# Attention scores in pairs of units, and the probabilities' products at the end of their position

## What is computed

```python
q, k = _rope(_rms_norm(q, q_norm_w), _rms_norm(k, k_norm_w), cos, sin)
attn = jnp.einsum('bhqd,bhkd->bhqk', q, k) * scale
attn = jax.nn.softmax(jnp.where(causal, -jnp.inf, attn), axis=-1)
out = jnp.einsum('bhqk,bhkd->bhqd', attn, v)
x = _layernorm(x + out.transpose(0, 2, 1, 3).reshape(Bc, Tc, C) @ w_proj.T)
x = _layernorm(x + shared_expert(x) + two_of_eight_experts(x))   # abbreviated
```

## Time and profile before

| | us |
|---|---|
| Time, median of 3 runs | 952.51 |
| Time of the profiled execution | 957.52 |
| Its span from the first to the last instruction | 955.8 |
| Busy: PE / PEld / DVE / ACT / POOL | 896.0 / 693.3 / 576.6 / 615.3 / 457.2 |
| Sequences 1 to 6, from 79 us to 329 us | 250 |
| Rest after 370 us (last rows of attention's output, experts, output) | 586 |

### The profile page before, as it was taken

One profiled execution on the slowest core, in us unless ns is written; L12 is line 12 of the kernel. 1 busy time (PEld: TensorE's weight loads), 2 busy tenths in 40 slices (PEclk: granted clock), 3 DMA queues, 4 the chain that ended last, 5 costly groups with the idle time before them and its releaser, 6 DMA issues.

```text
span 955.8 us, 26112 instructions
## 1 busy us (share of the span) xinstructions
PE 896.0 (94%) x9049; PEld 693.3 (73%) x9050; DVE 576.6 (60%) x1152; ACT 615.3 (64%) x1060; POOL 457.2 (48%) x668
## 2 busy tenths in 40 slices
PE   4789999998999989999999999999999999999995
PEld 1444555555555546888889989989899889898885
DVE  8655698889888636784344444454444433428875
ACT  4788898888878766442656655556655453667753
POOL 5344557877878636572134444344434343412211
PEclk9799999999999989999999999999999999999998
DMA  5112223433212255567882122121212121248641
GB/s 175 67 68 95 94 101 106 158 114 135 101 58 84 69 176 194 202 204 266 267 292 74 50 67 70 52 68 55 67 56 67 46 68 47 74 145 269 214 160 44
DMA packets 68706, 112.76 MB, mean 118 GB/s; under 512 B 7728, under 2 KB 46000, under 8 KB 68496
## 3 DMA queue, kind: packets, MB, share of 16 engines
q1 hardware_dynamic: 51248, 77.32, 24.5%
q10 hardware_dynamic: 10896, 16.40, 5.9%
q0 software_dynamic: 6480, 17.97, 5.2%
HBM read 66.58 MB, written 45.08 MB: 117 GB/s over the span
## 4 chain that ended last, share of the span: by engine, by line
PE 76%; ACT 7%; DVE 6%; issue 4%; POOL 2%; DMA 2%; another core or an unknown queue 1%; ACTq 1%; DVEq 0%; SPq 0%; POOLq 0%
PE hb L1811 23%; PE yb L1827 23%; PE pv_bank L1599 6%; PE slot L1577 4%; PE ma L1612 4%; PE slot L1586 3%; PE hb L1665 3%; ACT prob L872 2%; PE mb L1747 2%; PE ma L1622 1%; PE tr L1685 1%; DMA rs<-resid 1%; PE yb L1702 1%; PE mb L1735 1%
## 5 line engine op out<-in xcount | busy, mean ns | idle before, releaser
L1042 ACT ACTIVATE hf<-hb,b 128x256 f32<-128x256 f32 (+1 forms) x392 | 155.0, 454 | 206.2 <-PE hb L1811 200.7
L1811 PE MATMUL hb<-xgT,wts 128*128 128x256 f16 (+1 forms) x1872 | 213.2, 263 | 1.4 <-ACT hf L1042 1.2
L1827 PE MATMUL yb<-wts,hh 128*128 x1704 | 210.5, 273 | 0.9 <-DVE hh L1454 0.9
L1454 DVE TENSOR_TENSOR hh<-hf,hh 128x1024 f16<-128x1024 f32 (+1 forms) x98 | 120.2, 1229 | 137.3 <-ACT hh L1047 105.4
L1811 PEld LDWEIGHTS hb<-xgT,wts 128*128 x1872 | 181.2, 98 | 20.3 <-ACT hf L1042 1.0
L807 POOL DMA_INDIRECT y_tok<-yb,dest x71 | 77.8, 1096 | 227.0 <-DVE yb L1466 216.9
L1827 PEld LDWEIGHTS yb<-wts,hh 128*128 128x128 f16 x1704 | 166.3, 98 | 19.6 <-DVE hh L1454 1.2
L872 ACT ACTIVATE prob<-slot 128x1024 f32<-128x1024 f32 x160 | 161.6, 1034 | 27.8 <-PE slot L1586 27.3
L1047 ACT ACTIVATE hh<-hf 128x1024 f16<-128x1024 f32 (+1 forms) x98 | 97.6, 996 | 3.1
L741 POOL DMA_INDIRECT xg_rows<-xnh,sl_i x64 | 76.4, 1194 | 16.2 <-issue 13.9
L1577 PE MATMUL slot<-stk 64*128 64x128 f16 (+3 forms) x512 | 64.2, 308 | 16.2 <-ACT prob L872 11.6
(11 more groups left out here) (236 smaller groups left out, 1445.0 us busy)
## 6 DMA issues: line engine op xcount, KB each, us to landing
wts<-in_w_all SPq DMA_DIRECT2D x23, 512.0 KB
wts<-y_tok SPq DMA_DIRECT2D x32, 256.0 KB, 4.9
xg<-xg_rows ACTq DMA_DIRECT2D x30, 264.0 KB
stage<-in_w_all SPq DMA_DIRECT2D x12, 512.0 KB
w_split<-chunk_hl SPq DMA_DIRECT2D x12, 512.0 KB
xTf<-in_xT SPq DMA_DIRECT2D x8, 512.0 KB, 3.8
xin<-in_x SPq DMA_DIRECT2D x8, 512.0 KB
resid<-y SPq DMA_DIRECT2D x16, 256.0 KB
```

Source lines behind the costliest of these rows:

```text
L1042: act.activation(hf[:, c, 0:size], hb[c // 2][:, (c % 2) * TT:(c % 2) * TT + size], ACT.Relu, bias=bias, scale=1.0 / WS).then_inc(S("relu_ ...
L1454: dve.tensor_tensor(hh[:, par, 1, cs, 0:size], hf[:, cs, 0:size], hh[:, par, 0, cs, 0:size], ALU.subtract).then_inc(S("h_lo"), 1)
L1811: ins = pe.matmul(hb[hc // 2][:, (hc % 2) * TT:(hc % 2) * TT + size], weights(e, c, w, hc * P, P), xgT[:, par, x * DC + c, 0:size], start= ...
L1827: ins = pe.matmul(ybank[par][:, j * D:(j + 1) * D], hh[:, par, x, hc, P * j:P * j + P], weights(e, DC + hc * D // CH, w, hc * D % CH, D), ...
```

## The change

Three things are moved, and nothing is added or removed.

- On TensorE, at an even position p, the scores of the units p and p + 1 are written one after the other, and then the masks of both. At odd positions there is no unit.
- On ScalarE, at an even position p, the exponentials of p and p + 1 are written one after the other, ahead of the copies of p.
- `attended` on TensorE stands after all other jobs of its position.

```diff
                 def step(g):
                     for c, p in due(UNITS, g):
-                        exps(c, p)
+                        if p % 2 == 0:
+                            exps(c, p)
+                            exps(c, p + 1)
                     for c, i in due(AV, g - 1):
                         attended(c, i)
...
-                def scores(b, p):
+                def blocks(p):
...
+                def scores(b, p):
...
-                    for n, (pr, j, col) in enumerate(jobs):
+                    for n, (pr, j, col) in enumerate(blocks(p)[0]):
...
+                def masked(p):
+
+                    slot, diag = slots[p % 2], blocks(p)[1]
                     for x in range(2):
                         out = slot[:, 512 * x:512 * x + 512][:, diag[1]]
...
-                        scores(c, p)
-                    for c, i in due(AV, g):
-                        attended(c, i)
+                        if p % 2 == 0:
+                            for k in (p, p + 1):
+                                scores(c, k)
+                            for k in (p, p + 1):
+                                masked(k)
                     for c, t in due(TR, g):
                         stacked(c, t)
...
+                    for c, i in due(AV, g):
+                        attended(c, i)
```

More of the change, by code:

```diff
@@ L1557, in _ @@
                 pieces = [(x, y, c) for c in range(DC) for x, y in ((0, 0), (0, 1), (1, 0))]
+                def blocks(p):
+                    g, u = p // 5, p % 5
+                    if u in (0, 2):
+                        return [(2 * g + u // 2, 0, 0)], (1, slice(0, P))
+                    if u in (1, 3):
+                        return [(2 * g + u // 2, 3, 0), (2 * g + u // 2, 1, P)], (2, slice(0, 2 * P))
+                    return [(2 * g, 2, 0), (2 * g + 1, 2, 256)], (2, slice(0, 512))
                 def scores(b, p):
-                    g, u = p // 5, p % 5
                     par = b % 2
@@ L1566, in scores @@
                     slot = slots[p % 2]
-                    if u in (0, 2):
-                        jobs, diag = [(2 * g + u // 2, 0, 0)], (1, slice(0, P))
-                    elif u in (1, 3):
-                        jobs, diag = [(2 * g + u // 2, 3, 0), (2 * g + u // 2, 1, P)], (2, slice(0, 2 * P))
-                    else:
-                        jobs, diag = [(2 * g, 2, 0), (2 * g + 1, 2, 256)], (2, slice(0, 512))
-                    for n, (pr, j, col) in enumerate(jobs):
+                    for n, (pr, j, col) in enumerate(blocks(p)[0]):
                         for x in range(2):
@@ L1579, in scores @@
                                       stk[rows, par, 0, pr, P * j:T], start=(n == 0), stop=False, skip_group_check=True)
+                def masked(p):
+                    slot, diag = slots[p % 2], blocks(p)[1]
                     for x in range(2):
                         out = slot[:, 512 * x:512 * x + 512][:, diag[1]]
-                        if u == 4:
+                        if p % 5 == 4:
                             out = out.rearrange("p (i q) -> p i q", i=2)[:, :, 0:P]
```

## The result

The changed kernel takes 955.19 us (median of 20 runs, 952.4 to 959.6), the kernel before in the same group 951.62 (20 runs). The ratio is 1.0038, with a 95% interval of 1.0027 to 1.0048: slower by 3.6 us, where 4 us less were forecast. The profiled execution took 955.21. One of the six executions of a later kernel (single units in sequence 0, scatters later) took 2293 us and is left out of its median.

A forecast was written before the change was run, and what follows sets the result against it. TensorE was taken as the bound, three engines close behind. Per sequence 2.3 us saved less 1.6 lost, put at 0.8 for six sequences (4.8), less 1 for sequences 0 and 7: some 4 us off 952.5, 948.5 us; range 939.5 to 960.

The forecast's parts named there:

- The cost of a change of tiling: On TensorE: going from the whole array into another tiling costs 0.10 us, the way back 0.11 us.
- the pairs' saving: On TensorE in the attention: 10 x 0.11 + 12 x 0.10 = 2.3 us saved for each sequence.
- ScalarE's price in a sequence: Waits of TensorE at pairs 4, 6, 10 and position 18, plus 0.1 elsewhere: 1.6 us lost for each sequence.
- Six sequences alike at 0.8: Sequences 1 to 6 of the attention: each saves 0.8 us, 4.8 us together.
- VectorE's waits swallow the rest: TensorE's four waits for DVE, 5.5 us in all, swallow whatever ScalarE makes late in front of them.
- Sequences 0 and 7 at 1 us: First and last sequence: TensorE isn't the bound, the pairs delay ScalarE's copies; 1 us lost for the two.
- A saving buys nothing: Sequences 0 and 7: TensorE isn't the bound there, so its saving shortens nothing.
- the slower case: Whole kernel slower, beyond the 0.2% or 1.9 us that a measurement can tell from no change; chance 0.28.
- rival 2: Attention comes out even: waits, with places held by DVE and POOL, eat the 2.3 us; 952.5 us, chance 0.16.
- rival 3: ScalarE's copies, one exponential (0.97 us) later, lengthen the loop through DVE: 962 us, half of it 957; chance 0.28.
- The signs: If right: full sequences 41 to 43 us, TensorE's exponential waits 17 to 20 us, `stk` waits at every sequence's start.

## Why the prediction was wrong

- **The cost of a change of tiling and the pairs' saving: right.** Worked out 2.3 us a sequence, measured 2.4 where nothing else binds. The Trainium skill, TensorEngine Tiling (Array Packing), Key Properties, says that a change of mode drains the engine, and the 2.4 us agree with a cost for each change. The Trainium skill, TensorE: Matmul & The Clock Gate, Step-by-step, gives about 128 cycles for a matmul's last column to leave the array; taken as the whole price of a change, that is an estimate of 0.05 us, and half of the saving. Sequence 1 shows twice as much, so as a price of the change it is too low.
- **ScalarE's price in a sequence, 1.6 us: right in size, with one place wrong.** In sequence 2 TensorE's idle time rises from 1.13 (41.48 - 40.35) to 2.54 us (41.11 - 38.57), 1.4. Pair 4 doesn't wait; pairs 6 and 10 and unit 0 do, as said. But TensorE's busy time prints only 1.8 us less; against the 2.3 us saved the price is 1.9. Net 0.37 us instead of 0.7 to 0.8.
- **Six sequences alike at 0.8, and VectorE's waits swallow the rest: the step that failed.** The prediction counted TR ahead of the products only as a gain, since ScalarE's 1.61 us of idling there would go. It never asked whether `nat` is ready 2.36 us sooner. It wasn't: before, `nat` had been done 0.05 us when TR started, and the loop from `y` to `nat` took 14.5 us with and without the change, so that nothing saved on TensorE ahead of TR could bring TR forward. The earlier trace rows had a hint: of the 5.5 us for `an`, 3.3 are the same loop in the sequences 3, 4 and 6, seen from NAT behind the products, and 2.2 belong to the disturbed stretch of sequence 7. Against 0.8 us saved in each, the sequences came out at -0.1 and -0.4 us (1 and 2, where ScalarE's waits were dearer than taken), +1.1 and +0.4 (3 and 4), -0.4 and -0.5 (5 and 6); the forecast saving of 4.8 us became a loss of 0.1. Of these 4.9 us, 3.1 are missing in the sequences 3 and 4, and there the prediction had put a second thing at nothing: the granted clock fell behind the long wait. That is 1.1 us of sequence 3, which takes 42.69 us where it didn't fall, against 42.70 before (last section). In sequence 4 TensorE is busy for 1.5 us more than in sequence 2 (40.11 and 38.57); how much of it is in the length, no run shows.
- **Sequences 0 and 7 at 1 us: mis-sized.** Sequence 0 alone costs 3.8 us (46.32 - 42.55). "A saving buys nothing" was right; what the second exponentials delay wasn't added up there. TensorE waits for 12.1 us in it instead of 8.3: for exponentials 5.8 instead of 4.1, QK for V's copy 2.4 instead of 2.0, V for that of QK 2.0 instead of 0.6, unit 0 for `stk` 1.9 instead of 1.6. Single units there bring all of it back. Sequence 7 can't be read, as the profile of before is disturbed there.
- **The rivals.** By its time the result is the slower case, at which the prediction had put 0.28. In the sequences 1 to 6 the end is rival 2's (even, longer waits for the loop), and in sequence 0, where it wasn't looked for, a part of rival 3 (copies one exponential later). In the loop of full sequences rival 3's late copies aren't needed for the waits: with single units and ScalarE in its old order, products last alone has 8.3 us of waits for `nat`. What the late copies cost there beside it, no run has priced by itself. The sum now: +3.8 for sequence 0, +0.1 for 1 to 6, 3.9 against 3.6 measured, from one profile of each.
- **The signs.** Sequences of 41 to 45 us, TensorE's waits for exponentials 16.1 us in 26 places (17 to 20 forecast), `stk` at each start, and 7.8 us for `nat`, which stood as rival 3's sign, though the late copies aren't what made them.

## What to carry to other kernels

Before a job is moved forward in a queue, ask when its input is ready, not only who waits for its output; the work that it overtakes had been its cover, and now stands behind its wait. A bound engine's saving counts only in those stretches that no loop over the other engines closes, so cost each stretch (here the first sequence, those without routing, those with it) by itself, and look for the loop behind the small waits. And where waits grow, look whether the granted clock falls behind them: with products last only, that made 5.0 of the 6.6 us that the sequences 3 and 4 took more. Here the change was worth making only with two others, single units in the first sequence and the scatters later: 0.5% faster than before, and neither the pairs (even with single units in sequence 0) nor the scatters' move gained alone.

## What the runs showed of the hardware

- Behind some waits of 2.3 to 2.5 us TensorE's clock fell for a few us: after the wait of 2.42 us at 178.14 the granted clock was 0.59 on average from 178 to 182 us, between the two levels of 1.2 and 2.4 GHz, and the sequence showed 0.96. That was worth 1.1 us: the same sequence with the same wait of 2.42 us and no fall, in the kernel with sequence 0 single, took 42.69 us (clock 1.00) against 43.80. It didn't fall each time: there it fell only behind the next wait, of 2.51 us. Nor does it take one long wait: with pairs only, three of 1.34, 1.03 and 0.52 us between 183.5 and 188 us were followed by 0.59 as well, while before, waits of 1.41 and 0.38 us in the same place left the clock at 1.00. The rows: after, 178 to 182 us; pairs only, 188 to 192 us; and sequence 3 of the kernel with sequence 0 single.

```profile
178.00:182.00 4.00, 3.86 (x32) 2.76 (x36) 3.86 (x6) 1.20 (x2) 3.53 (x5) 0.59 0.31 118
```

```profile
188.00:192.00 4.00, 4.00 (x33) 3.00 (x35) 3.00 (x8) 4.00 (x7) 2.98 (x3) 0.59 0.41 146
```

```profile
165.83:208.52 42.69, 38.51 (x458) 24.19 (x456) 36.60 (x87) 36.29 (x57) 34.19 (x46) 1.00 0.34 113
```

- A change from the whole array to 64 rows costs 0.10 us and back 0.11, and in pairs one of each is saved for every two units; two units took 0.32 + 0.12 and 0.33 + 0.23 us one by one and take 0.54 + 0.34 in a pair.
